# Attention and gated FFN over selected tokens: another order of the units, and the values of four heads in one block

## The reference

```python
x = x + _L0_xcond_ref(cond_1024, ctx_1024, _layernorm(x), ...)
x = x + _L0_ffn_ref(_layernorm(x), ...)
...
scores = x @ w_router
_, idx = jax.lax.top_k(scores, CAP)
x_sel = jnp.take_along_axis(x, idx[:, :, None], axis=1)
h = rmsnorm(x_sel, g1)
q, k, v = (h @ W_qkv.T) split into 16 heads of 32
att = softmax(where(mask, -inf, q @ k.T / sqrt(32)))
x_attn = (att @ v) @ W_out.T
h2 = rmsnorm(x_sel + x_attn, g2)
x_ff = silu(h2 @ W1.T) * (h2 @ W2.T) @ W3.T
out = x.at[idx].set(x_sel + x_attn + x_ff)
```

## Time and profile before

| | us |
|---|---|
| median of 3 runs | 2549.41 (2543.11 to 2551.65) |
| the profiled execution | 2548.73 |
| its span, first to last instruction | 2547.0 |
| PE matmuls busy | 2364.5 (93% of the span) |
| DVE / ACT / POOL busy | 1603.7 / 976.0 / 1056.9 |
| mean granted TensorE clock | 0.968 of full |

### The profile page before, as it was taken

One profiled execution on the slowest core, in us unless ns is written; L12 is line 12 of the kernel. 1 busy time (PEld: TensorE's weight loads), 2 busy tenths in 40 slices (PEclk: granted clock), 3 DMA queues, 4 the chain that ended last, 5 costly groups with the idle time before them and its releaser, 6 DMA issues. The chain is left out here.

```text
span 2547.0 us, 31016 instructions
## 1 busy us (share of the span) xinstructions
PE 2364.5 (93%) x11492; PEld 1918.5 (75%) x11492; DVE 1603.7 (63%) x2932; ACT 976.0 (38%) x1646; POOL 1056.9 (41%) x1528
## 2 busy tenths in 40 slices
PE   7988799999999999999899999989999987897997
PEld 3776688888877888887788888778888866665786
DVE  5777755747656585767557476755757776644442
ACT  0455423333332433342243333324333335564331
POOL 0455505244271624436263453636345377443200
PEclk9899999999999999999999999999999998998999
DMA  3566200000033000012400001240000121104230
GB/s 120 204 242 242 85 1 1 1 1 1 34 113 144 5 21 5 18 42 106 151 5 21 5 9 50 100 157 5 21 5 9 51 83 50 34 24 118 75 116 17
DMA packets 87782, 158.59 MB, mean 62 GB/s; under 512 B 12233, under 2 KB 34761, under 8 KB 84558
## 3 DMA queue, kind: packets, MB, share of 16 engines
q1 hardware_dynamic: 83238, 150.26, 17.1%
q0 software_dynamic: 2944, 6.31, 0.8%
q10 hardware_dynamic: 1450, 0.04, 0.0%
HBM read 106.21 MB, written 50.38 MB: 61 GB/s over the span
## 5 line engine op out<-in xcount | busy, mean ns | idle before, releaser
L211 PE MATMUL ps<-zTh,kTl 128*128 128x512 f32 (+1 forms) x912 | 336.9, 369 | 26.8 <-ACT prob L1678 22.8
L213 PE MATMUL ps<-zTh,kTh 128*128 128x512 f32 (+1 forms) x912 | 328.4, 360 | 0.0
L212 PE MATMUL ps<-zTl,kTh 128*128 128x512 f32 (+1 forms) x912 | 328.2, 360 | 0.0
L211 PE MATMUL ps<-vh,prob_lo 128*128 128x512 f32 x768 | 307.3, 400 | 11.5 <-DVE prob_lo L2049 11.5
L213 PE MATMUL ps<-vh,prob_hi 128*128 128x512 f32 x768 | 300.2, 391 | 0.0
L212 PE MATMUL ps<-vl,prob_hi 128*128 128x512 f32 x768 | 299.3, 390 | 0.0
L1834 DVE TENSOR_TENSOR zTl<-ps,zTh 128x512 fp32r<-128x512 f32 x224 | 151.1, 684 | 230.7 <-ACT zTh L1559 230.7
L2210 POOL TENSOR_SCALAR rs_m<-mv_m 128x1 f32<-128x1 f32 x96 | 39.6, 412 | 610.4 <-DVE mv_m L1768 608.4
L1678 ACT ACTIVATE prob<-ps,nb 128x1024 f32<-128x1024 f32 x96 | 107.3, 1118 | 298.2 <-DVE nb L2072 298.2
L211 PEld LDWEIGHTS ps<-zTh,kTl 128*128 128x128 f32 x912 | 174.6, 191 | 61.2 <-ACT prob L1678 26.5
L1541 ACT ACTIVATE zbuf<-slots,rs_m 128x512 f32<-128x512 f32 x96 | 78.4, 816 | 344.5 <-POOL rs_m L2214 344.5
(11 more groups left out here) (308 smaller groups left out, 5754.7 us busy)
## 6 DMA issues: line engine op xcount, KB each, us to landing
ctx<-in_ctx_dram SPq DMA_DIRECT2D x8, 1024.0 KB, 11.6
slots<-in_x_dram SPq DMA_DIRECT2D x8, 1024.0 KB, 11.9
kT_d<-kTh SPq DMA_DIRECT2D x6, 1024.0 KB, 4.5
kT_d<-kTl SPq DMA_DIRECT2D x6, 1024.0 KB, 6.8
s_d<-slots SPq DMA_DIRECT2D x6, 1024.0 KB, 4.4
v_d<-vh SPq DMA_DIRECT2D x6, 1024.0 KB, 6.4
v_d<-vl SPq DMA_DIRECT2D x6, 1024.0 KB, 9.3
kTh<-kT_d SPq DMA_DIRECT2D x3, 2048.0 KB, 10.4
```

Of the source, the lines that this page charges most:

```text
L211: nc.tensor.matmul(out, ll, rh, start=start, stop=False)
L212: nc.tensor.matmul(out, lh, rl, start=False, stop=False)
L213: return nc.tensor.matmul(out, lh, rh, start=False, stop=stop)
```

## The change

1. **Order of the units.** The table `UNITS` and all five lists are written anew, from the last slot round to the third FFN chunk. By step (n = 8q + i), what PE makes beside the pairs:

| steps | before | now |
|---|---|---|
| ahead of 0 | Q(0) x8, V(0,0), scores(0), V(0,1), scores(1) | Q(0) x3, scores(0), Q x2, scores(1), Q x3, V(0) x2 |
| 0 to 7 | T(1) at 1, Q(1) two a step at 2 to 5, V(1) at 6, 7 | T(1) at 0, Q(1) one at 1, two at 2, 3, V(1) at 4, 5, Q(1) at 6, 7 |
| 8 to 15 | T(2) at 8, O(0) at 9, Q(2) two a step at 10, 11, N(0) and Q at 12, Q x3 at 13, V(2) at 14, 15 | T(2) at 8, Q(2) at 9, O(0) at 10, Q x2 at 11, 12, Q at 13, V(2) at 14, 15 |
| 16 to 23 | O(1) at 17, T(3) at 19, N(1) and Q(3) at 20, Q x3 at 21, four Q and V at 22, V at 23 | Q at 16, N(0) at 17, O(1) at 18, Q at 19, T(3) at 20, Q(3) at 21, 22, V(3) at 23 |
| 24 to 31 | O(2) at 25, N(2) at 28, up(0) at 29, 30 | Q(3) at 24, 25, N(1) at 25, O(2) at 26, up(0) at 29, 30, up(1,0) at 31 |
| behind 31 | values, up(1), O(3), down(0), up(2), N(3), down(1), wait, up(3) | values, down(0), up(1,1), O(3), down(1), up(2), up(3), ...; N(2) in chunk 4, N(3) in chunk 6 |

2. **First scores at the third unit.** Queries and keys come in turn (`QE`), and `scores` of a batch waits for as many units as it reads, not for all eight. ACT reads the units first and normalises the gathered rows after.
3. **Values of four heads.** `values` runs once for two pairs, ahead of `turn` in every even step, first the four heads' 256-column matmuls, then their 128-column ones.
4. **Last slot round.** POOL splits the gelu's outputs ahead of `row_scale(0)`; DVE turns the low part (`m_lo(7)`) ahead of the last count in the rounds that rank (g = 5, 8, 11), and makes `h_lo(0)` ahead of the round's last two residuals; ACT casts wv and wo in this round.
5. **The last batch's scores.** `score` and `base` are spread over steps 1 to 7 (before 0 to 4), the counts over steps 9 to 13 (before 7 to 11), the scatter over 13 to 15 (before 12 to 14), `gather(3)` in step 17 (before 16).
6. **End.** The last down of each half signals each bank by itself (`ff_tile`), and `add_ffn` adds it at once. The FFN's weights are loaded after the last Q too.

The diff, cut:

```diff
+    QE = (0, 4, 1, 5, 2, 6, 3, 7)
+    N_AFTER = {4: B - 2, 6: B - 1}
...
         sp.wait_ge(sem("vq_done"), B * QT)
+        sp.wait_ge(sem("qk_done"), B * 8)
...
-            if i == 0:
-                pe.wait_ge(sem("qk_read"), q * 8 + 8)
+            if i % 2 == 0:
+                pe.wait_ge(sem("qk_read"), q * 8 + i + 2)
...
-        def values(n):
-
-            q, i = divmod(n, HP)
-            pe.wait_ge(sem("pT_ready"), n + 1)
-            if i == 0:
+        def values(c):
+
+            q, e = divmod(c, EB)
+            pe.wait_ge(sem("pT_ready"), 2 * c + 2)
+            if e == 0:
                 pe.wait_ge(sem("vq_read"), q * QT + QT)
-            if n >= 2 and n % 2 == 0:
-                pe.wait_ge(sem("o_split"), n // 2)
-            for g in range(2):
-                h = 2 * i + g
-                r = 32 * (h % 4)
-                cs = cut(h, HD)
-                p_ = pT[:, n % 2, g, :]
-                out = bank(4)[r:r + HD, :]
-                nc.tensor.matmul(out[:, 0:CAP], vt[q % 2][:, 0, cs], p_[:, 0:CAP], start=True, stop=False)
-                last = nc.tensor.matmul(out[:, P:CAP], vt[q % 2][:, 1, cs], p_[:, CAP:], start=False, stop=True)
-            last.then_inc(sem("o_done"), 1)
+            if c >= 1:
+                pe.wait_ge(sem("o_split"), c)
+            for k in range(2):
+                for h in range(4):
+                    p_ = pT[:, h // 2, h % 2, :]
+                    out = bank(4)[32 * h:32 * h + HD, :]
+                    cs = cut(4 * e + h, HD)
+                    if k == 0:
+                        nc.tensor.matmul(out[:, 0:CAP], vt[q % 2][:, 0, cs], p_[:, 0:CAP], start=True, stop=False)
+                    else:
+                        last = nc.tensor.matmul(out[:, P:CAP], vt[q % 2][:, 1, cs], p_[:, CAP:], start=False, stop=True)
+            last.then_inc(sem("o_done"), 2)
...
+            if (m, k) == (0, 0):
+                pe.wait_ge(sem("h2_split"), 2 * QT)
+            if m == 0 or (m, k) == (1, 0):
+                x = last_unit(up_banks(m)[k])
+                pe.wait_ge(sem(unit_read(x)[0]), unit_read(x)[1])
+            if (m, k) == (1, 1):
+                pe.wait_ge(sem("o_split"), B * EB)
+            if m == 2:
+
+                pe.wait_ge(sem("y_ready"), TL + k + 1)
+            if m - 1 in N_AFTER and k == 0:
+                pe.wait_ge(sem("hf_ready"), (N_AFTER[m - 1] + 1) * QT)
...
-        V(0, 0)
+                if ch == FC - 1:
+                    last.then_inc(sem("ff_tile"), 1)
+                elif t == HT - 1:
+                    last.then_inc(sem("ff_done"), 1)
+
+        Q(0, 0); Q(0, 1); Q(0, 2)
         scores(0)
-        V(0, 1)
+        Q(0, 3); Q(0, 4)
         scores(1)
+        Q(0, 5); Q(0, 6); Q(0, 7)
+        V(0, 0); V(0, 1)
         for n in range(PAIRS):
             q, i = divmod(n, HP)
...
+            if n >= 2 and n % 2 == 0:
+                values(n // 2 - 1)
+            turn(n)
...
+                    O(2, 1)
+        values(B * EB - 1)
+        down(0)
         up(1, 1)
         O(3, 0); O(3, 1)
-        down(0)
+        down(1)
         up(2, 0); up(2, 1)
-        N(3, 0); N(3, 1)
-        down(1)
-        pe.wait_ge(sem("hf_ready"), B * QT)
...
+                N(N_AFTER[m], 0); N(N_AFTER[m], 1)
             down(m - 1)
...
             for c in range(C):
                 A.activation(wv[0][:, c, :], wv_st[:, c, :], ACT.Copy, scale=g1c[:, c:c + 1]).then_inc(sem("w_hi"), 1)
+            A.activation(wo[0][:, :, :], wo_st[:, :, :], ACT.Copy).then_inc(sem("w_hi"), 1)
...
-        values_hi()
+        for u in range(6):
+            qk_out(0, u)
+        exps(0)
+        qk_out(0, 6); qk_out(0, 7)
         norm_gathered(1)
-        for u in range(4):
-            qk_out(0, u)
-        final_norm(B - 1, 0)
-        qk_out(0, 4); qk_out(0, 5)
-        final_norm(B - 1, 1)
-        exps(0)
...
-            dve.wait_ge(sem("ff_done"), h * FC + FC)
             for t in range(HT):
+                dve.wait_ge(sem("ff_tile"), h * HT + t + 1)
                 V.tensor_tensor(x1g[:, h * HT + t, :], bank(t), x1g[:, h * HT + t, :], ALU.add)\
                     .then_inc(sem("fo_ready"), 1)
...
+        gathered_stats(1)
+        dve.wait_ge(sem("pool_step"), 4 + 4)
+        masked_max(0)
         for c in range(C):
...
             rstd("f", (B - 1) * NT + j, j)
-            if j >= 2:
-                base(B - 1, j - 2)
-
+
+        row_scale(1)
         scatter(B - 2, range(NT // 2, NT))
-        row_scale(1)
+        normalise(0)
         for j in range(3):
             final(j)
-        pool.wait_ge(sem("tok_in0"), 2 * 16)
-        gather(2)
-        final(3)
-        normalise(0)
...
+                if i == 1:
+                    base(B - 1, 0)
+                    final(4)
...
-                count(6); count(7)
-                if b and t == ROUNDS - 1:
+                count(6)
+                ranks = b and t == ROUNDS - 1
+                if ranks:
+                    m_lo(7)
+                count(7)
+                if ranks:
                     rank_tokens(b - 1)
                 if last:
-                    m_lo(7)
                     residual(0); gained(0)
                     residual(1)
...
                     rstd_p(0); rstd_p(1)
+                    split_gelu(1, 0); split_gelu(1, 1)
+                    rstd_p(2)
+                    split_gelu(1, 2)
+                    rstd_p(3)
+                    split_gelu(1, 3)
                     row_scale(0)
-                    rstd_p(2)
-                    split_gelu(1, 0)
-                    rstd_p(3)
-                    split_gelu(1, 1); split_gelu(1, 2); split_gelu(1, 3)
                     scatter(b - 1, range(NT // 2))
```

More of the change, by code:

```diff
@@ L271, in unit_before, with last_unit @@
         return next((y for y in reversed(UNITS[:k]) if UNIT_BANK[y] == UNIT_BANK[x]), None)
+    def last_unit(k):
+        return next(y for y in reversed(UNITS) if UNIT_BANK[y] == k)
     def yrow(tt):
@@ L342, in Q @@
             for c in range(C):
-                last = mm3(pe, bank(UNIT_BANK["Q", q, u])[:, 0:CAP], pair(wqk, ALL, c, cut(u)), pair(hT, ALL, c, ALL),
+                last = mm3(pe, bank(UNIT_BANK["Q", q, u])[:, 0:CAP], pair(wqk, ALL, c, cut(QE[u])), pair(hT, ALL, c, ALL),
                            c == 0, c == C - 1)
@@ new lines, in routed_pe @@
+            if q == 1:
+                if i == 2:
+                    O(0, 0)
+                if i in (3, 4, 5):
+                    Q(2, 2 * i - 5)
+                if i in (6, 7):
+                    V(2, i - 6)
+            if q == 2:
+                if i == 0:
+                    Q(2, 6)
+                if i == 1:
+                    N(0, 0)
+                if i == 2:
+                    O(1, 0)
+                if i == 3:
+                    Q(2, 7)
+                if i == 4:
+                    T(3, 0)
+                if i == 5:
+                    Q(3, 0)
+                if i == 6:
+                    Q(3, 2)
+                if i == 7:
+                    V(3, 0)
@@ new lines, in routed_pe @@
+            if q == 3:
+                if i < 2:
+                    Q(3, 2 * i + 4)
+                if i == 2:
+                    O(2, 0)
+                if i in (5, 6):
+                    up(0, i - 5)
+                if i == 7:
+                    up(1, 0)
+            if n >= 2 and n % 2 == 0:
+                values(n // 2 - 1)
+            turn(n)
+            if q < 2 and i == 0:
+                T(q + 1, 1)
+            if q < 2 and i == 1:
+                Q(q + 1, 0)
+            if q == 0:
+                if i in (2, 3):
+                    Q(1, 2 * i - 2)
+                if i == 7:
+                    Q(1, 7)
@@ L739, in routed_act @@
[L739 to L758 removed]
+                    qk_out(3, 3)
@@ L784, in routed_act @@
+        act.wait_ge(sem("tr_h2"), 2 * QT)
+        norm_again(2)
         split_hi(RING)
-        gate_and_split(2)
-        again_hi(3)
-        for m in range(3, CHUNKS):
-            gate_and_split(m)
+        for m in range(2, CHUNKS):
+            gate(m)
+            if m in N_AFTER:
+                again_hi(N_AFTER[m])
+            if m + RING - 1 < CHUNKS:
+                split_hi(m + RING - 1)
+            if m == 4:
+                act.wait_ge(sem("tr_h2"), TL)
+                norm_again(3)
@@ L897, in routed_dve @@
                                    ALU.mult, ALU.subtract).then_inc(sem("w_split"), 1)
-        gathered_stats(1)
-        def final(j):
+        masked_max(1)
+        invert(0)
+        dve.wait_ge(sem("row_in"), 3 * 16)
+        for j in range(3):
             final_stats(B - 1, j)
-            if j >= 2:
-                scores(B - 1, j - 2, tbuf[:, 0, :])
-        def count(j):
-            if j == 0:
-                dve.wait_ge(sem("score_in"), B * 16)
-            count_tokens(B - 1, j, last_row[:, :], zbuf[:, :, :].rearrange("p r d -> p (r d)"), tbuf[:, 1, 0:P])
-        dve.wait_ge(sem("row_in"), 3 * 16)
```

(9 more changed lines are left out.)

478 lines of the change are left out of this document (229 added, 249 removed).

## The result

| | before | changed |
|---|---|---|
| median of the runs shown with the result | 2548.47 (2543.11 to 2551.65, 4 runs) | 2518.69 (2516.68 to 2522.09, 4 runs) |
| ratio | | 0.9887 (0.9866 to 0.9907) |
| span of the profiled execution | 2547.0 | 2515.0 |

29.8 us less in the medians, 32.0 in the spans; 38 was forecast, in a range of 12.7 to 56.7 (2511 us, and 2492 to 2536). In the 14 profiles of this study the last slot round's first down product comes between 2043.9 and 2053.2 us, whatever the kernel, and the first slot round's between 416.7 and 424.9, so a span alone blurs a difference of some us. From here on times are therefore measured in each trace **from the last slot round's first down product** (`ps<-w2h,gT0l`, at 2052.1 us before and 2052.9 after) **to the end**: 494.9 us before, 462.1 after, 32.8 less. I call that the routed time.

A forecast was written before the change was run, and what follows sets the result against it. The prediction took the phase to be bound by PE plus single waits, 63.6 us of them. Its terms summed to -46.4, and with 8 added for hidden chains the forecast was -38, 2511 us, range 2492 to 2536.

The forecast's parts named there:

- PE's waits, round, ramp and steps 0 to 7: Last slot round to step 7: earlier splits and reads shorten PE's waits, -13.3; steps 0 to 7 add +1.
- steps 8 to 15: DVE stands still 9 to 11 us ahead of the first count; PE's waits 11 instead of 8.1 us, +2.9.
- steps 16 to 23: POOL's scatters delay turns and `gather(3)`'s chain delays T(3); PE's waits 10 instead of 5.2 us, +4.8.
- step 24 to up(3): FFN work fills the ends of the pairs' chain and N(3) moves to chunk 6; 4.5 us of waits left, -17.9.
- end: Kernel's end: banks added as they end, one add stays behind the last matmul and the write starts earlier, -2.5.
- values: PE's values blocks: four heads overlap, so 16 blocks of 0.79 us instead of 32, -12.6.
- `m_lo(7)`: Rounds g = 5 and g = 8: earlier low part, about 0.7 us gained in each, less the rounding, -1.
- clock: Stretches with granted clock 0.80 to 0.97: with less idle time the clock loss falls from about 25 to 18, -7.
- added for hidden chains: The 32 steps: shorter steps expose chains the old trace hides, ends of 0.2 to 0.3 us a step, +8.
- filled with PE's work: Steps 0 to 7: PE's own work, 4.7 us a step, fills them, +1 (0 to +6).
- first rival: The 32 steps: a pair's chain binds; slower from a mean step of 7.5 us, 2565 us at 8; chance 5%.
- Granted clock above 0.9 everywhere: A sign expected in the changed kernel's profile, from the first scores on.

The follow-up runs named there:

- e2: The kernel before with values blocks of four heads alone: median 2551.67 against 2549.69 us, ratio 1.0009, routed time 500.0 against 494.9.
- e5: The changed kernel with every values block made twice, 12.6 us more PE work: median 2518.88 us, routed time 466.9, +4.8.
- e11: The changed kernel with `m_lo(7)` behind the last count again in rounds g = 5 and g = 8: median 2514.59 us.
- e8: The changed kernel with scores written in halves, row load ahead of the last four bases, those made in steps 8 to 11: 2507.89 us, routed time 454.5.
- e12: e8 with `h_lo(2, .)` ahead of step 9's work, `split_lo(0)` a mask later and `squares(2)` behind `o_lo` on DVE: 2501.65 us, routed time 447.7.
- e4: The changed kernel with first scores behind all eight units of Q(0), which ACT reads before the first exponentials: 2522.52 us, routed time 467.6, +5.5.
- e9: The kernel before with ACT reading all eight units of Q(0) ahead of its normalising: ratio 0.9984, median 6.4 us lower, routed time 491.2.
- e10: The kernel before with N(3) in chunk 6 of the FFN: ratio 0.9973, median 7.2 us lower, routed time 489.8.
- e6: The changed kernel with POOL's old order in the last slot round, `row_scale(0)` and `rstd_p(2)` ahead of the gelu splits: 2513.7 us, routed time 462.2.
- e7: The changed kernel with POOL's `final(1)` and `final(2)` behind `normalise(1)` instead of ahead: 2513.81 us, routed time 461.7, -0.4.

## Why the prediction was right, and where not

| term | forecast | in the profiles |
|---|---|---|
| PE's waits, round, ramp and steps 0 to 7 | -12.3 | 27.0 to 18.2: -8.8 |
| steps 8 to 15 | +2.9 | 8.2 to 10.2: +2.0 |
| steps 16 to 23 | +4.8 | 5.3 to 9.2: +3.9 |
| step 24 to up(3) | -17.9 | 22.3 to 9.1: -13.2 |
| add in the middle | -0.8 | 0 |
| end | -2.5 | -2.0 |
| values | -12.6 | block 0.79 as said, worth 0 (e2) to 4.8 (e5) |
| `m_lo(7)` | -1 | 0 (e11) |
| clock | -7 | some -4 to -5 (first 300 us: mean 0.89 to 0.91) |
| added for hidden chains | +8 | 7.0 us of waits more than forecast |

In the routed time the parts close: PE's waits 63.6 to 47.3 us (-16.3, forecast -23.3), PE's busy time 418.0 to 403.5 (-14.5, forecast -19.6 for values and clock), behind PE's last matmul -2.0 (forecast -2.5); together -32.8. The +8 made good the waits, and what is missing to the forecast is PE's busy time. The two are not apart: made twice, the blocks take 5.7 us of the waits away again (e5), so a large part of the +8 was the values' gain coming back as waits, and not a cost of its own.

The direction, the range and many marks were right: first exponential at 2111.8 (2114 forecast), turn(0) at 2120.1 (2118), the block at 0.79, DVE's 11.2 us ahead of the count with 4.2 on PE, nothing at up(3). Three marks were missed: PE's waits (47.3 us, near 40 forecast), the step (6.3 us, 5.2 to 5.6 forecast) and the clock (below). The ramp's sum was met with luck: its waits came to 13.3 us where 13.8 was forecast, but `gT1l` took 5.6 of them instead of 2.5 and T(0)'s `hn` 0.6 instead of 3.6. The 8 us added for "chains that the old trace hides" were there, and the trace now names them: 3.9 in steps 0 to 7, where POOL was full (38.25 of 42 us), `row_scale(2)` and `final(6)` stood ahead of the probabilities of turn(6), which waited 1.8 us, and `base(4)` and `final(7)` ahead of those of turn(7), which waited 3.1 (1.8 in e8, without that base); and 4.7 in the last steps, of which the 4.2 us for the mask behind `split_lo(0)` is the most (0.9 in e12, which moves it). The prediction had read POOL's load nowhere for the new steps: PE was busy 4.8 us a step from turn(0) to turn(7), as it said (4.7), but a step took 6.0, so "filled with PE's work" was wrong. (In its first rival the "some 44" is 46.3 by its own terms for ramp, tail, end and values, which moves that rival's time by 2 us.)

**The step that failed is the term of the values.** Its size on PE was exact (16 blocks fewer of 0.79 us), and its worth was not: 0 to 4.8 us where 12.6 was forecast. The prediction added idle time taken away and PE work taken away as if each were worth its length. e2 shows 12.6 us of work turned into 12.6 us of waits, and e5 that the new order gives 4.8 for them. The rule weighed in the prediction (the Trainium skill, "TensorEngine Tiling (Array Packing)", section "PSUM Bottleneck"), that the copies out of PSUM may take the gain, gave the right number in the old order, but not because the engines that copy were full: DVE and ACT were 60% and 52% busy there (179.0 and 155.5 of 300 us). What PE waited for more was masks of DVE and probabilities of POOL. That they came late by their place in the lists is argued, not tested in the old order.

What of the 32.8 is tested in isolation: third unit 5.5 (e4), reads first 3.7 (e9), N(3) 8.1 behind turn(31) (e10), values up to 4.8 (e5); these were taken in two orders, so they add only roughly. The trace alone shows 2.0 at the end. The rest, some 9 us (the masks ahead of the statistics on DVE, V(0) behind the first scores, the spread of steps 24 to 31), was not undone one by one. The ramp's parts stand in series: ACT's order alone gave 5.5 of the 15.4 us at turn(0), the third unit 4.0, POOL's order in the slot round none.

"Granted clock above 0.9 everywhere" was wrong: 0.87 and 0.83 from step 8 to step 23, with 19.4 us of waits there where the old order had 13.5. The clock's term came out at some -5: what is missing to 1 in 300 us fell from 33 to 27 us, and PE is busy 81 to 85% of that time. PE's busy time says much the same: it fell by 14.5 us, of which e5 gives the blocks 10.4 (413.9 against 403.5), and 4.1 are left for the clock and all else. Both are estimates, since the old order's own clock differs by 0.02 from profile to profile.

## What to carry over

Before PE work is priced at its length, ask how long its next operand takes to appear; where other engines set that, less work becomes more waiting (e2), and doubling the work (e5) measures its price in one run. A wait's own length was its worth where one engine set the pace (e10, 8.1 us for a wait of 6.3); in a chain over four lists it was not (e6 made one wait 4.5 us longer at no cost, e7 made one 2.5 shorter and gained 0.4), so count from landmark to landmark there. And look first at how far two profiles of the same code lie apart in that stretch: 3.0 us up to turn(31) in the old order (before and e10), 0.2 behind it (before and e9). When a change fills steps evenly, add up every engine's new load per step, not only that of the engine that bounds.

## What the runs showed of the hardware

Four heads of 32 columns in partition groups of their own take the time of two, 0.79 us, and 0.81 in another order of issue. Writing the 1024 scores, 4 bytes each, to HBM took 13.9 us from issue to the next transfer in the changed kernel and 12.2 and 10 to 11 us for half of them, so it is mostly a time that halving doesn't touch. And the granted clock moved without the sum of the waits: 0.89 and 0.87 in two profiles of the same code in the old order, 0.91 in e8 and 0.94 in e12, whose waits are only 1.7 us shorter. What in the pattern of the waits decides it, no run here shows.
